# Feed-forward stage: the x2 normalisation on VectorE as tensor times column plus a column read with a step of zero

## What is computed

```python
t = _to_tokens(x)                       # 36864 tokens of 128 channels
t = t + _L0_ffn_ref(_ln_t(t), ...)

def _ln_t(v, eps=1e-05):
    m = jnp.mean(v, axis=-1, keepdims=True)
    s = jnp.var(v, axis=-1, keepdims=True)
    return (v - m) / jnp.sqrt(s + eps)

def _L0_ffn_ref(x, ...):
    logits = jnp.mean(x, axis=1) @ Wr + br          # one pair of experts for all tokens
    ...
    h = gelu(x @ W1[e] + b1[e])                     # 128 -> 256 for each of the two experts
    y = h @ W2[e] + b2[e]
    out = sum over the two experts of weight * y
    return _layer_norm(out + x, gamma, beta)
```

## Time and profile before

| | |
|---|---|
| median of 3 runs | 1425.35 us (1424.94 to 1429.03) |
| span of the profiled execution, first to last instruction | 1419.6 us |
| the profiled execution's own time | not listed apart from its span; the median of the runs is 5.75 us above the span |
| TensorE busy | 1344.6 us, 95% of the span |
| VectorE busy | 1216.5 us, 86% |
| GpSimd busy | 999.5 us, 70% |
| ScalarE busy | 1001.3 us, 71% |

### The profile page before, as it was taken

How to read it: one execution, slowest core, us unless ns; L and a number is a source line. 1 busy time by engine, 2 the same in 40 slices (tenths; PEclk the granted TensorE clock), 3 DMA queues, 4 the chain that set the end, 5 groups by cost and what they waited for, 6 DMA issues and landing times. The chain is left out here.

```text
span 1419.6 us, 32205 instructions
## 1 busy us (share of the span) xinstructions
PE 1344.6 (95%) x9880; PEld 1129.9 (80%) x9880; DVE 1216.5 (86%) x4125; ACT 1001.3 (71%) x2327; POOL 999.5 (70%) x1559
## 2 busy tenths in 40 slices
PE   6999999999999997999799999699999999999994
PEld 3877788877888777999666667599999999999984
DVE  7998899989989884888799998667888888888997
ACT  3888888888888886565467776346677766776773
POOL 4999999999999996444388888334555555655574
PEclk9999999999999999999899999799999999999997
DMA  9999999999999999788699995211222232222213
GB/s 218 229 252 253 254 249 251 258 255 254 243 255 258 257 243 296 269 293 306 169 281 301 300 300 177 94 45 51 84 75 75 75 87 78 75 77 79 84 45 89
DMA packets 357530, 267.48 MB, mean 188 GB/s; under 512 B 60432, under 2 KB 332722, under 8 KB 357362
## 3 DMA queue, kind: packets, MB, share of 16 engines
q1 hardware_dynamic: 355800, 264.76, 70.0%
q10 hardware_dynamic: 1290, 0.46, 0.2%
q0 software_dynamic: 272, 0.21, 0.1%
HBM read 171.02 MB, written 94.37 MB: 187 GB/s over the span
## 5 line engine op out<-in xcount | busy, mean ns | idle before, releaser
L1558 ACT ACTIVATE hT<-psH_d,b 128x512 f32<-128x512 f32 x288 | 197.9, 689 | 154.7 <-PE psH_d L1598 154.6
L675 PE MATMUL psZ_a<-w_all,xT_a 128*128 128x128 f32 x1728 | 229.9, 276 | 0.0
L675 PE MATMUL psZ_a<-w_all,xT_block 128*128 128x384 f32 x576 | 214.0, 495 | 5.2 <-DVE low_ab L744 5.1
L675 PEld LDWEIGHTS psZ_a<-w_all,xT_a 128*128 128x128 f32 x1728 | 209.8, 192 | 2.3 <-ACT xT_a L583 2.1
L599 ACT ACTIVATE sig_a<-psZ_a 128x256 f32<-128x256 f32 (+1 forms) x360 | 153.8, 427 | 79.2 <-PE psZ_a L675 49.5
L611 POOL TENSOR_SCALAR shared<-shared,coefs_early 128x128 f32<-128x128 f32 x468 | 204.7, 460 | 0.0
L662 PE MATMUL psT_a<-ident,shared 128*128 128x128 f32 x1152 | 186.1, 274 | 3.7 <-issue 2.1
L662 PEld LDWEIGHTS psT_a<-ident,shared 128*128 128x128 f32 x1152 | 141.0, 142 | 54.9 <-issue 26.7
L1252 DVE TENSOR_SCALAR shared<-shared,coef 128x128 f32<-128x128 f32 x288 | 179.2, 681 | 1.6 <-POOL xh_b L1632 1.6
L1625 POOL TENSOR_TENSOR u_d<-u_d,gamma 128x512 f32<-128x512 f32 x72 | 94.1, 1307 | 117.4 <-ACT u_d L1541 116.0
L1632 POOL TENSOR_TENSOR xh_b<-shared,b 128x512 f32<-128x512 f32 x72 | 93.5, 1298 | 105.0 <-DVE ffn_sum L1693 103.8
(11 more groups left out here) (234 smaller groups left out, 3165.1 us busy)
## 6 DMA issues: line engine op xcount, KB each, us to landing
shared<-in_x_dram SPq DMA_DIRECT2D x48, 512.0 KB, 5.7
scratch_xT<-xT_block SPq DMA_DIRECT2D x36, 512.0 KB, 5.2
shared<-scratch_xT SPq DMA_DIRECT2D x36, 512.0 KB, 5.0
scratch_x<-x_c SPq DMA_DIRECT2D x36, 512.0 KB, 4.0
shared<-scratch_x SPq DMA_DIRECT2D x36, 512.0 KB, 3.4
shared<-in_x_dram SPq DMA_DIRECT2D x48, 256.0 KB, 5.2
shared<-L_conv_protein_pair_dram SPq DMA_DIRECT2D x24, 512.0 KB, 6.8
shared<-in_L_conv_l_pair_dram SPq DMA_DIRECT2D x24, 512.0 KB, 9.1
```

Of the source, the lines that this page charges most:

```text
L675: ins = nc.tensor.matmul(out, turned_x(G, i, t0, size)[:, j * P:j * P + P], rhs[i], start=True, stop=True)
L1558: nc.scalar.activation(hT[:, S % 2, f, :], psH[:, f, :], ACT.Gelu, bias=s["b1"][:, f:f + 1]).then_inc(gelued, 1)
```

## The change

One line, in `norm_x2`. The two-column instruction (multiply by one column, add another column) becomes one that multiplies by a column and adds a second tensor; that tensor is the same column, read 128 times by a step of zero along the row.

```diff
     t = 4 * g + i
     r, b = (s["coef_2"][:, q, bass.ds(TPB * n + t, 1)] for q in range(2))
-    ins = nc.vector.tensor_scalar(s["xh_d"][:, g % 2, i, :], s["x2"][:, t, :], r, b, ALU.mult, ALU.add)
+    ins = nc.vector.scalar_tensor_tensor(s["xh_d"][:, g % 2, i, :], s["x2"][:, t, :], r, b.broadcast_to([P, CH]), ALU.mult, ALU.add)
     if i == 3:
         ins.then_inc(s["normed_d"], 1)
```

## The result

The changed kernel takes 1427.61 us (median of 20 runs), the kernel before 1424.47 us (20 runs): ratio 1.0023, 95% interval 1.0016 to 1.0030, thus 2.3 to 4.3 us more, by the middle 3.3. The forecast was 1427.4 us and +2.1 us, "the same". The median is inside the range, and the change lies inside the 0.3% that was called no change, but with 20 runs of each it is a small loss and no longer nothing.

A forecast was written before the change was run, and what follows sets the result against it. TensorE, busy throughout the slots, was taken to bound the kernel. Thirteen places x 0.14 = 1.8 us, 0.3 for the last slots and 0.04 ahead of the slots gave +2.1 us on 1425.35: 1427.4 us, range 1423.5 to 1432.

The forecast's parts named there:

- TensorE bounds the slots, VectorE counts at thirteen places: TensorE is full; its products wait for VectorE's split at nine places once in six slots and four in the last slots.
- Nowhere else: Outside the thirteen places, extra VectorE time costs nothing: plain slots have about 1 us of waiting per slot.
- The new form is held as the old one is: In L1252's groups, GpSimd's L1632 and L1636 hold the two-tensor form exactly as the old one; group 2.46 to about 2.60 us.
- The rival by which a step of zero is no second tensor: At L1252 nothing is held, a group falls to 1.1 us; -4.0 us, 1421.4 us in total; chance 0.09.
- +0.06 us for each of two held instructions: Once let go, a held L1252 ends 0.15 us behind GpSimd instead of 0.09; together +0.12 us per group of four.
- +0.01 us for a free one: Each of the two L1252 instructions per group that are not held takes 0.01 us longer, +0.02 us per group.
- Nine places x 0.14 = 1.26 us: Once in six slots, the third group's extra 0.14 us reaches TensorE; the first two groups' extra is absorbed by held steps.
- The last four places, 4 x 0.14 + 0.3 = 0.86 us: In the last slots, 0.14 us per place, plus 0.3 for a third held instruction or a chain step falling elsewhere.
- the turned L1708: In the last slots, one L1708 falling behind GpSimd's L1625 and being held: up to 1.5 us more, in the range only.
- the second rival: At the nine places L1708 falls behind the gamma product L1625, 1.5 us more each; 1439 us in total; chance 0.10.
- Ahead of the slots +0.04 us: The first four tiles ahead of the slots stand on the path and cost 4 x 0.01 us.

The follow-up runs named there:

- the dense tile: Changed kernel's new form in all 288 places, but with a dense tile of ones as second tensor instead of the step-of-zero column; ratio 1.0020 to the kernel before.

## Why the prediction was right, and where it was off

- *TensorE bounds the slots, VectorE counts at thirteen places.* Right: the new form at 57 groups, among them all plain slots, has a ratio of 0.9993; at the other fifteen groups it has 1.0019. The plain slots keep 6.77 us in every profile. "Nowhere else" was a little too strong: at two places the extra of the group ahead came through as well, 0.25 us together.
- *The new form is held as the old one is.* Right: mean 0.711 us forecast "about 0.71"; without GpSimd in the way 0.367. The rival by which a step of zero is no second tensor is excluded by the dense tile, 711 ns as well. The Trainium skill, SBUF — State Buffer, § Who interferes with whom, has two SBUF inputs held by GpSimd's reads; these runs agree, 0.711 us with GpSimd in the way against 0.367 without. "Exactly as the old one is" holds only for GpSimd instructions that read, which all are that run beside L1252 in this kernel; a memset holds the old form and not the new one.
- *+0.06 us for each of two held instructions.* Right in its parts: 0.15 us behind the end of GpSimd's instruction was worked out, 0.15 and 0.14 were measured; the group grew by 0.12, where the sum had 0.14.
- *+0.01 us for a free one.* Measured 0.007. The prediction's estimate from the Trainium skill, VectorE: DVE Perf Modes, § The perf-mode tier table, 64 cycles more for the form that takes one element per cycle, would have made it 0.067; the distance of 0.263 us against 0.256 does not show it. The old form reads two columns and the new one only one; that this is what cancels is worked out from the rows, not shown by a run.
- *Nine places x 0.14 = 1.26 us.* Measured 1.40 us in the profile. The difference sits at two places (0.27 us at the second, 0.26 at the last), where the group ahead was not absorbed either: its own L1666 came 0.10 us ahead of TensorE, too. The new form at the other groups alone costs 0.14 and 0.11 us at just these two.
- *The last four places, 4 x 0.14 + 0.3 = 0.86 us.* This is the term that was mis-sized: 1.35 us. The prediction kept the turned L1708 for the upper end of the range ("up to 1.5 more if one L1708 in the last slots is turned"); the runs show that it is the rule, in the four profiles with the new form there and GpSimd's order as it was, by 0.05 to 0.08 us. The prediction let a chain's step that is held end when L1625 ends, whenever it began; but which step is held depends on when VectorE comes, L123 before and L121 in all four, and the 0.22 us of that and the group's 0.13 together used up the 0.27 us that the pair had. The prediction had both terms, 0.14 and 0.2 us, and added them up without comparing the sum with this margin. The mechanism of the second rival was thus real, at one place and not at nine: at the nine the margin fell from 0.38 to 0.26 us at the first, and to 0.11 us at the last.
- *Ahead of the slots +0.04 us.* From the first L1252 to TensorE's first L1596 for group 2 the profile is shorter by 0.36 us, but over all profiles this stretch is 18.4 to 19.5 us long, and both ends of the range occur with the new form. The clock is at its lower level when it begins (0.50 from 905 to 910 us, before and after) and at the higher one when it ends, and the moment of the change differs from profile to profile. No effect of the change can be read there.
- The sum of +2.1 us against +2.4 us in the profile and +3.3 us (2.3 to 4.3) by the runs: the direction and the mechanism stand; the size was a third too small by the runs and an eighth by the profile, which lies inside their interval.

## What to carry to other kernels

Here a mean duration twice the shortest one was a queue, not work. So find in the two timelines which instruction of the other engine ends just before, and the time of a new form follows from the two ends, not from its rate. Where another engine is full, count the places at which it waits and multiply by those; here 60 of 288 instructions carried nearly all of the cost. Where the margin between two instructions that exclude each other is about as long as the change (0.08 us decided over 1.1 us), look up which place has the least margin (0.27 us here), and add up everything that makes one engine late there, because the turned order, not the added time, is then the price.

## What the runs showed that I had not expected

- The last slots answer to tenths of a microsecond in jumps of either sign: the new form at nine earlier groups made a wait of 1.48 us into 0.35 us, and at the last six groups it made a new one of 1.33 us. Moving GpSimd's additions there moved the waits and did not remove them.
- A wait of TensorE of 1.82 or 1.90 us was followed by a few microseconds at the lower clock in two of the eleven experiments' profiles, which cost 1.6 us each (0.57 of full speed on average in 4 us); a wait of 1.84 us before left the clock at 1.00. Why is open.
- The two forms are not held alike in all cases, against the prediction's "exactly as the old one is". An addition of GpSimd holds both; a memset, which only writes, holds the old form (it ends 0.08 us behind) and not the new one (0.34 us, done before the memset is). There the form with two tensors was the faster one, 2.19 us for eight against 2.88.
- Making GpSimd wait for VectorE, with the new form, is the one version whose interval lies below the kernel before (0.9979 to 0.9997, 1.7 us by the medians); with the old form it does not (0.9986 to 1.0005), though the two profiles' slots are equal within 0.3 us. So a gain of about 2 us is what the profiles show, and the runs confirm it for one of the two only.
